# Attention with experts on one Trainium2 core: the wide form of the vector engine's exponentials in 25 units instead of 14, each expert spread over two units

## The reference

```python
xn = layernorm(x)                          # x: 16 batches x 256 tokens x 128
Q, K, V = xn@Wq+bq, xn@Wk+bk, xn@Wv+bv     # 16 heads of 8
for wl in range(16):                       # the scan over wavelengths
    c = cos(phase[wl])                     # one number for each head
    s = (Q*c) @ (K*c).T * SCALE            # then s * cos(KERR*s*s); KERR is 2.7e-12
    acc += softmax(s) @ V * weights[wl]
attn = (acc/16) @ Wo + bo
e = argmax(softmax(xn @ gate_w.T))         # one expert of 8 for each token, capacity 640
ffn = prob * (relu(xn @ w1[e] + b1[e]) @ w2[e] + b2[e])
out = x + attn + ffn
```

## Time and profile before

| | |
|---|---|
| median of three runs | 1749.12 us (1748.42 to 1751.1) |
| profiled execution, its own time | 1749.12 us |
| profiled span, first to last instruction | 1747.4 us |
| ACT busy | 1698.0 us, 97% of the span |
| DVE busy | 1550.1 us, 89% |
| PE busy | 1523.0 us, 87% |
| POOL busy | 215.1 us, 12% |
| DMA, mean | 28 GB/s |
| mean granted TensorE clock | 0.995 |

### The profile page before, as it was taken

One profiled execution on the slowest core, in us unless ns is written; L12 is line 12 of the kernel. 1 busy time (PEld: TensorE's weight loads), 2 busy tenths in 40 slices (PEclk: granted clock), 3 DMA queues, 4 the chain that ended last, 5 costly groups with the idle time before them and its releaser, 6 DMA issues.

```text
span 1747.4 us, 47074 instructions
## 1 busy us (share of the span) xinstructions
PE 1523.0 (87%) x20698; PEld 967.4 (55%) x20698; DVE 1550.1 (89%) x2310; ACT 1698.0 (97%) x517; POOL 215.1 (12%) x246
## 2 busy tenths in 40 slices
PE   6988978898888899999999998888888888887888
PEld 4454545555555566666666655555555555555555
DVE  5579799999998999999999998899999888998796
ACT  4999999999999999999999999999999999999996
POOL 4407000122110000000000000244430000000000
PEclk8999999999999999999999999999999999999999
DMA  3300000110001111011110000000000000000000
GB/s 123 101 16 16 15 11 25 53 52 24 26 10 36 37 44 44 15 30 44 44 44 23 15 10 15 26 25 26 26 10 15 15 15 15 16 12 6 2 28 26
DMA packets 45827, 49.70 MB, mean 28 GB/s; under 512 B 7565, under 2 KB 38325, under 8 KB 45621
## 3 DMA queue, kind: packets, MB, share of 16 engines
q1 hardware_dynamic: 42176, 42.11, 7.8%
q0 software_dynamic: 2048, 4.20, 0.8%
q10 hardware_dynamic: 1396, 0.33, 0.1%
HBM read 30.50 MB, written 15.73 MB: 26 GB/s over the span
## 4 chain that ended last, share of the span: by engine, by line
ACT 75%; PE 18%; DVE 3%; issue 3%; DMA 1%; SPq 0%; POOL 0%; DVEq 0%
ACT Pr L1426 73%; PE bank L1204 10%; PE bank L978 2%; ACT Pr L1419 2%; PE bank_b L1381 1%; PE bank L1354 1%; PE bank L1135 1%; DVE negmax L1125 0%; DVE T L1141 0%; DMA base<-in_L_attn_x_dram 0%; PE bank L1119 0%; PE bank L621 0%; PE bank L586 0%; PE bank L561 0%; PE bank L502 0%
## 5 line engine op out<-in xcount | busy, mean ns | idle before, releaser
L1426 ACT ACTIVATE Pr<-T 128x4096 f32<-128x4096 f32 x463 | 1628.6, 3604 | 12.1 <-PE bank L1204 11.2
L1204 PE MATMUL bank<-Pr,Vst 128*32 128x256 f32 x14912 | 901.3, 382 | 183.9 <-ACT Pr L1426 101.1
L1204 PEld LDWEIGHTS bank<-Pr,Vst 128*32 128x32 f32 x14912 | 497.2, 109 | 469.6 <-issue 266.7
L1125 DVE TENSOR_REDUCE negmax<-bank 128x2 f32<-128x512 f32 x248 | 159.1, 683 | 58.1 <-PE bank L1119 57.6
L1141 DVE COPY T<-bank 128x512 f32<-128x512 f32 x248 | 168.9, 684 | 19.1 <-PE bank L1135 17.0
L1381 PE MATMUL bank_b<-terms,ident 128*128 128x128 f32 x992 | 144.0, 278 | 0.3 <-DVE terms L1366 0.3
L1347 DVE TENSOR_SCALAR pv_s<-bank,row_scale 128x512 f32<-128x512 f32 x192 | 142.2, 741 | 0.9 <-PE bank L1204 0.8
L1381 PEld LDWEIGHTS bank_b<-terms,ident 128*128 128x128 f32 x992 | 126.1, 192 | 12.0 <-issue 8.6
L1354 PE MATMUL bank<-ident,pv_s 128*128 128x128 f32 x768 | 117.3, 275 | 3.4 <-DVE pv_s L1347 3.3
L1362 DVE RECIPROCAL rsum<-bank 128x48 f32<-128x48 f32 (+1 forms) x192 | 79.9, 416 | 35.9 <-PE bank L1354 35.7
L1366 DVE TENSOR_TENSOR terms<-bank,rsum 128x384 f32<-128x384 f32 (+1 forms) x192 | 98.6, 513 | 6.6
(11 more groups left out here) (251 smaller groups left out, 1392.5 us busy)
## 6 DMA issues: line engine op xcount, KB each, us to landing
Ks<-qk_parts SPq DMA_DIRECT2D x30, 288.0 KB
Qs<-qk_parts SPq DMA_DIRECT2D x90, 96.0 KB
qk_parts<-work SPq DMA_DIRECT2D x12, 384.0 KB, 2.9
work<-in_L_ffn_w_dram SPq DMA_DIRECT2D x16, 256.0 KB, 3.8
dispatched<-d_both SPq DMA_DIRECT2D x5, 512.0 KB, 6.1
region<-dispatched SPq DMA_DIRECT2D x8, 320.0 KB, 3.8
expert_out<-work SPq DMA_DIRECT2D x8, 320.0 KB, 3.0
out_dram<-base SPq DMA_DIRECT2D x8, 256.0 KB, 3.0
```

What stands on the lines that cost most here:

```text
L1125: nc.vector.reduce_max(negmax[par][:, ds(p * QT, QT)], sc_bank[rr][:, :].rearrange("p (t k) -> p t k", k=SEQ), AX.X, negate=True).then_inc ...
L1204: ins = nc.tensor.matmul(bank[VC * j:VC * (j + 1), half * SEQ:(half + 1) * SEQ], Vst[par][:, at:at + VC], moving, start=opens and half == ...
L1426: nc.scalar.activation(Pr[n % RING][:, :], T[par][:, :], ACT.Exp, scale=scales[u % 2][w]).then_inc(exp_done, 1)
```

## The change

Four things change together.

- `x_bank` is split: `side_bank` for the experts and the output projection, `wide_bank` for the passes of all wide units.
- All units from 6 to 30 are wide (`WIDES`), with or without an expert: 25 in place of 14. New are 9, 10 to 17, 29 and 30.
- An expert is spread over two units (units 10 to 25 in place of 10 to 17). `expert_step` says which piece stands in which step: eight pieces in the first unit, seven in the second, in some steps alone, and no piece in the others. With one bank, PE waits before every piece until DVE has read the piece before.
- Gather and combination move from units 19 to 22 to units 26 to 29 (`CU`), and the output of side 0 waits for the first two of four combinations alone.

```diff
+        side_bank, wide_bank = x_bank
...
-                pe.wait_ge(x_read, e * EI + (X0 + w - 1 if w else X0))
+                pe.wait_ge(x_read, e * EI + (X0 + w))
...
-                    dve.wait_ge(base_ready, CHUNKS)
+                    dve.wait_ge(base_ready, CHUNKS // SIDES * (n // NQ_SIDE + 1))
...
             def pe_pass(pe, u, i, final):
-                bank = x_bank[u % 2]
...
-                    pe.wait_ge(pv_copied, (u - 1) * GROUPS + 2)
-                    pe.wait_ge(x_read, X0 if u < EU else XO)
+                    pe.wait_ge(pv_copied, u * GROUPS + 2)
+                    pe.wait_ge(x_read, X0)
...
+            CU = EU + 2 * E
+            EXPERT_AT = ({0: 0, 2: 1, 4: 2, 5: 3, 6: 4, 10: 5, 13: 6, 15: 7}, {0: 8, 2: 9, 5: 10, 6: 11, 10: 12, 13: 13, 15: 14})
+            def expert_step(u, w):
+                e, half = divmod(u - EU, 2)
+                return e, EXPERT_AT[half].get(w)
...
-            KINDS = ([FIRST, NORM, SIDE, ROUTE, QKV, QKV] + [WIDE] * (EU - 7) + [PLAIN] + [EXPERT] * E
-                     + [WIDE] * (UNITS - 3 - EU - E) + [PLAIN] + [FINAL] * 2)
+            KINDS = ([FIRST, NORM, SIDE, ROUTE, QKV, QKV] + [PLAIN] * (EU - 6) + [EXPERT] * (2 * E)
+                     + [PLAIN] * (UNITS - 2 - CU) + [FINAL] * 2)
+            WIDES = [u < UNITS - 1 and k in (PLAIN, EXPERT, FINAL) for u, k in enumerate(KINDS)]
...
                 for e in range(E):
-                    unit(EU + 1 + e, (e + 1) % 2, e, next_expert=e + 2 < E)
+                    unit(EU + 1 + 2 * e, 1)
+                    unit(EU + 2 + 2 * e, 0, e, next_expert=e + 2 < E)
```

More of the change, by code:

```diff
@@ L1233, in pe_pass @@
                 for kt in range(tiles):
-                    ins = wide_product(pe, bank, w, half, kt, V, lambda j, blk: source[:, (j * tiles + kt) * SEQ:(j * tiles + kt + 1) * SEQ],
+                    ins = wide_product(pe, wide_bank, w, half, kt, V, lambda j, blk: source[:, (j * tiles + kt) * SEQ:(j * tiles + kt + 1) * SEQ],
                                        opens=(i, final, kt) == (0, 0, 0), closes=bool(last and kt == tiles - 1))
@@ L1345, in dve_products @@
                 dve.wait_ge(turned, u * GROUPS + q + 1)
-                bank = x_bank[u % 2] if q == GROUPS - 1 and KINDS[u] == WIDE else pv_bank[q % 2]
+                bank = wide_bank if q == GROUPS - 1 and WIDES[u] else pv_bank[q % 2]
                 nc.vector.tensor_scalar(pv_s[q % 2][:, :], bank[:, :], row_scale[:, q:q + 1], None, ALU.mult).then_inc(pv_copied, 1)
@@ L1497, in attention_and_experts @@
             LONG_BEFORE = before([W - (c > 0) - (u == 0) for u, c in enumerate(D_CHUNKS)])
-            D_OPS_BEFORE = before([POPS * len(PIECES) if k == WIDE else DOPS * c for k, c in zip(KINDS, D_CHUNKS)])
-            WIDE_BEFORE = before([k == WIDE for k in KINDS])
+            D_OPS_BEFORE = before([POPS * len(PIECES) if wide else DOPS * c for wide, c in zip(WIDES, D_CHUNKS)])
+            WIDE_BEFORE = before(WIDES)
             WHOLE_BEFORE = before([c == ALL_CHUNKS for c in D_CHUNKS])
@@ L1545, in step @@
                         pe_products(pe, u, par, 2 * W - 3 - w)
-                    elif w == W - 2 and kind == WIDE:
+                    elif w == W - 2 and WIDES[u]:
                         pe_rest(pe, u)
@@ L1549, in step @@
                         pe_products(pe, u, par, w)
-                    if w == 0 and u and KINDS[u - 1] == WIDE:
+                    if w == 0 and u and WIDES[u - 1]:
                         pe_pass(pe, u - 1, len(PIECES) - 1, 1)
@@ L1585, in step @@
                     elif kind == EXPERT:
-                        pe_expert(pe, u - EU, (u - EU) // 2, par, w)
+                        e, i = expert_step(u, w)
+                        if i is not None:
+                            pe_expert(pe, e, e // 2, e % 2, i)
                     elif (u, w) in OUT_AT:
@@ L1667, in step @@
                     elif kind == EXPERT:
-                        dve_expert(dve, u - EU, par, w)
+                        e, i = expert_step(u, w)
+                        if i is not None:
+                            dve_expert(dve, e, e % 2, i)
                     elif (u, w) in OUT_AT:
@@ L1726, in unit @@
                                 pool_combine(pool, c // 2)
-                        if half == 0 and KINDS[u + 1] == WIDE:
+                        if half == 0 and WIDES[u + 1]:
                             if not WIDE_BEFORE[u + 1]:
@@ L1800, in plain_sync @@
                 for e in range(E):
-                    unit(EU + 1 + e, (e + 1) % 2, e, next_expert=e + 2 < E)
-                for u in range(EU + E + 1, 2 * LAST):
+                    unit(EU + 1 + 2 * e, 1)
+                    unit(EU + 2 + 2 * e, 0, e, next_expert=e + 2 < E)
+                for u in range(CU + 1, 2 * LAST):
                     unit(u, u % 2)
```

47 lines of the change are left out of this document (20 added, 27 removed).

## The result

The changed kernel took 1740.16 us (median of 5 runs, 1738.46 to 1742.01). The kernel before took 1749.12 beside it (5 runs, 1747.03 to 1753.97). The measured ratio is 0.9932 with a 95% interval of 0.9916 to 0.9948; the two medians by themselves give 0.9949. In a later series beside the experiments the change took 1741.37 (6 runs) against 1752.18, a ratio of 0.9948 (0.9930 to 0.9966). The prediction was 1737.5, its range 1736.0 to 1743.5.

What follows compares the result with a forecast made beforehand. ACT, busy 97% of the span, was taken to bound the kernel. Saving 9.4 us of quarter exponentials and 2.2 of waits, 11.6 together, takes 1749.12 to 1737.5 us; range 1736.0 to 1743.5.

Steps and rivals of the forecast that it cites:

- ACT sets the length, 51.78 in a wide unit: Units 9 to 17, 29 and 30 made wide at 51.78 us each, ACT without gaps: 11.6 us saved together.
- How late PE may be: At a unit's start, PE may begin a step's products 1.51 us behind the exponential's end before ACT loses time.
- End of a second unit: Ends of units 11, 13, ... 25: two more w2 pieces make PE 1.25 us late, under 1.51, margin 0.26.
- End of a first unit: w1 reads delay DVE's copy of group 4, making the next unit's step 0 products 0.95 us late, margin 0.56.
- PE 48.5 and 50.5, DVE 50.6 and 48.5 us busy in first and second units: Units 10 to 25, each with half an expert: both engines' work fits within the wide unit's 51.78 us.
- POOL's cover of 11.7 us in unit 30: V staged 43.7 us into unit 30, needed by unit 31's products at 55.4: 11.7 us to spare, costed at nothing.
- The failed term: unit 30: Unit 30 wide with the combination: DVE needs 47.6 of 51.8 us, so it fits; no change in unit 31.
- One bank makes PE stand: Rival, chance 0.03: PE waits for DVE's reads of expert pieces, 17.4 us in all, 1754.9 if ACT loses all.
- Part lost to PE: Rival, chance 0.20: ACT loses 0.32 us in each of units 10 to 25, 5.1 in all, giving 1742.6.
- Nothing gained: Rival, chance 0.05: ACT loses 0.73 us in each unit with half an expert, leaving 1749 us.
- DVE overflow: Rival, chance 0.04: each expert's 7.1 us of DVE lengthens its two units in full, 45 us more, 1794.
- the prediction's main case: Full saving of 11.6 us, chance 0.68, with its own range of 1736.0 to 1739.5 us.

Runs made afterwards that it cites:

- the doubled piece: The changed kernel with PE computing each expert's last w2 piece (step 15 of its second unit) twice, into the same place: 1748.05 us, one run.
- the gathers moved: The changed kernel with the gathers of units 26 to 29 issued earlier: 1743.8; one a step: 1741.1, profiled again 1742.99; that with unit 30 plain: 1743.32 us.
- whole experts: The changed kernel with all 15 pieces of an expert in its first unit and none in its second: 1762.03 us, one run.

## Why the prediction was right, point by point

- **ACT sets the length, 51.78 in a wide unit.** Right in all units from 7 to 29. Units 9 to 17 gave 9.85 of 9.90.
- **How late PE may be: 1.51 us.** Confirmed by two runs. Beside the doubled piece above, the plain units with spread experts give it: there the second exponential ended 3.51 before 801.15, at 797.64, the products of step 1 began 1.73 later, and 0.22 was lost.
- **End of a second unit: 1.25 late, margin 0.26.** Measured 1.00 (exponential from 790.29 to 793.89, products at 794.89), margin 0.51. A w2 piece adds less than its row because it overlaps its neighbours; in the doubled piece it was 0.89 and not 1.05.
- **End of a first unit: at most 0.95 late.** Measured 0.63 (842.07 + 3.60 = 845.67, products at 846.30).
- **PE 48.5 and 50.5, DVE 50.6 and 48.5 us busy in first and second units.** Measured 48.8 and 49.1, 47.6 and 49.2: PE's second units were priced too high, DVE's first ones too; DVE's second ones a little too low.
- **POOL's cover of 11.7 us in unit 30.** Right: V was staged by 1664.1, 45.3 us into unit 30, and nothing waited for it.
- **The failed term: unit 30.** "Unit 30 has 43.9 on DVE; 1.9 for wide and 1.8 for the combination make 47.6 of 51.8", and "I take no change" for unit 31. The sum was even too high (43.7), yet 0.45 and 1.15 were lost, 1.7 us in all with ACT's restarts. The walk through the tightest place, made for the ends of first and second units, was not made for unit 30, whose output reads go up to step 15 and have a matmul of PE behind them. The runs showed the causes: without the wide order 0.24 is left, without POOL 0.29, without output pieces (unit 29) nothing is lost, and when POOL holds up both DVE operations the gap of 0.45 grows to 2.25.
- **One bank makes PE stand.** PE did idle before w1 pieces for DVE's reads, 3.2 us in all in the eight experts (14 times), so the sign that the prediction named for this rival did show, but ACT lost nothing by it: the lateness borne covers it. The row of the Trainium skill that the prediction weighed ("PSUM — Partial Sum Buffer", Summary: rules for kernel authors) asks for a different bank and for a semaphore guard by bank. The change has the guard, so one bank was no mistake by that row, and here it cost 0 on the path.
- **The other rivals.** Part lost to PE: no gap in units 10 to 25. Nothing gained and DVE overflow: excluded by the same rows.
- **The rest of the distance to 1737.5.** Of 2.7, 1.7 is unit 30's and 31's; the remaining 0.9 lies within the set-up's spread.
- **The range.** 1740.16 lies above 1739.5, where the prediction's main case ended. It is inside the range by the stretch that was kept for a loss to PE in units 10 to 25. That loss did not come; units 30 and 31 and the set-up filled its place. So the mechanism was right for units 9 to 29, but that the range held the time was in part luck.

## What to carry to other kernels

A margin read from a small gap (a gap of 0.2 behind a lateness of 1.71 gives 1.51) is worth more than busy shares; it held to 0.01 us in two other kernels. But apply it in each kind of unit that a change touches, above all the least busy one: DVE was at 43.7 of 52 us in the only unit that lost. And two parts that are each worthless can be worth 10 us together, so undo them singly before crediting either.

## What the runs showed of the hardware

**Behind a short idle the clock can be halved, or not.** In the four profiles with the gathers moved, PE idled 1.59 us at 16 unit ends alike, and once more at the end of unit 30 with the output projection earlier. Behind five of the 17, one in each profile and not always at the same unit, products took 3.1 to 3.6 us in place of 1.93, at a granted clock of 0.57 to 0.61 in windows of 4 us, a mixture of 1.2 and 2.4 GHz; with the gathers moved each cost ACT about 1.2 to 1.6. Behind the other twelve the clock stayed at 1.00. In the change itself the unit ends from 6 to 29 have no such idle, and no fall. The length of the idle alone does not decide: one of 2.58 (output earlier) and one of 1.84 (last piece twice) brought no fall. What does was not found.

**The set-up shows the same fall.** The changed kernel's first profile, PE and then the granted clock in a window, in unit 0:

```profile
81.76 1.04 PE L1114 MATMUL bank<-Ks,Qs 72*128 72x256 bf16 x4 [3.53 <-DMA Qs<-qk_parts]
...
84.86 3.29 PE L1199 MATMUL bank<-Pr,Vst 128*32 128x256 f32 x32
```

```profile
82.00:86.00 4.00, 4.00 (x26) 3.11 (x28) 2.06 (x4) 1.17 (x1) 0.00 (x0) 0.50 0.31 108
```

and its second profile:

```profile
81.82 0.61 PE L1114 MATMUL bank<-Ks,Qs 72*128 72x256 bf16 x4 [1.41 <-DMA Qs<-qk_parts]
...
83.47 1.93 PE L1199 MATMUL bank<-Pr,Vst 128*32 128x256 f32 x32
```

```profile
82.00:86.00 4.00, 4.00 (x54) 2.70 (x56) 2.21 (x5) 3.89 (x2) 0.00 (x0) 1.00 0.36 123
```

The wait for one load was 3.53 in the one and 1.41 in the other. Behind the long one the clock was 0.50, the lower level throughout, and unit 0 took 68.0 instead of 63.3. But in the first profile unit 0 also began 1.9 earlier, and unit 2 gave 1.6 back (57.4 against 59.0), so at the start of unit 6 only 1.1 is left. Over all 13 profiles unit 6 starts between 371.5 and 377.4. How much of this is the clock is not shown, and the length of the wait does not decide here either: one of 2.24 (unit 30 plain again) left the clock at 1.00, one of 1.82 (whole experts) at 0.68. This spread of nearly 6 us, in code that no edit touched, is larger than what unit 30 is about, so the experiments are compared from unit 6 on.

**POOL and DVE wait for each other in whole operations, and the order of their starts decides who pays.** DVE's operation with two inputs in SBUF takes 2.28 us alone. In the change L1268 began 0.60 before POOL's first operation and kept its 2.28, and POOL's took 3.44. L1271 began while that one ran and took 3.39; it ended 2.15 behind POOL's end. With the last piece twice, POOL's first operation began 0.15 before L1268: POOL's took 1.90, L1268 3.89, again ending 2.14 behind POOL's. It is the same wherever these operations overlap, in all 13 profiles: DVE's wide operation, when second, ends 2.14 to 2.16 behind the end of POOL's, and POOL's two, when second, 1.75 to 1.77 and 2.23 to 2.26 behind DVE's, for starts 0.15 to 2.6 apart. So a shift of 0.7 us in POOL's start took DVE's loss in unit 30 from 1.1 to 3.2. In unit 30 plain, where DVE's operations are half as wide, POOL's two took 2.0 and 3.3. The Trainium skill's page "SBUF — State Buffer" (Who interferes with whom) says that a DVE instruction with two SBUF inputs contends with a GpSimd instruction that reads SBUF; these rows agree.
